# Another order of all engines' steps in a fused audio tower, with quad 0 as a token group of its own

## The reference, cut to what matters

```python
# token pooling: windows of 8 times, weighted by a softmax over the 8
scores  = einsum('bwkf,of->bwko', xp, w) + b          # xp: 128 x 94 x 8 x 64
pooled  = sum(xp * softmax(scores, axis=2), axis=2)   # 128 x 94 x 64
# attention, 8 heads, on layernorm(pooled)
q = einsum('btd,hrd->bhtr', x, Q);  k = einsum('bud,hrd->bhur', x, K)
attn = softmax(einsum('bhtr,bhur->bhtu', q, k) / sqrt(64))
out  = einsum('bhtd,hde->bte', einsum('bhtu,bud->bhtd', attn, x), VO)
# then an expert attention, causal, 4 heads x 4 experts of width 16,
# gated by a softmax over the experts, a small two-layer net per head
# between two normalisations, and a last gate over the heads
```

## Time and profile before

| | us |
|---|---|
| median of three runs (1001.07, 999.45, 999.99) | 999.99 |
| the profiled execution | 1001.54 |
| its span in the trace | 999.8 |
| a plain step in the middle, mix to mix | 27.0 |
| a step with a token score | 30.5 |
| from the start to the first `mix` | 56.0 |
| from the last `mix` to the end | 87.9 |

### The profile page before, as it was taken

One profiled execution on the slowest core, in us unless ns is written; L12 is line 12 of the kernel. 1 busy time (PEld: TensorE's weight loads), 2 busy tenths in 40 slices (PEclk: granted clock), 3 DMA queues, 4 the chain that ended last, 5 costly groups with the idle time before them and its releaser, 6 DMA issues.

```text
span 999.8 us, 39459 instructions
## 1 busy us (share of the span) xinstructions
PE 901.8 (90%) x16312; PEld 615.8 (62%) x16312; DVE 803.9 (80%) x1836; ACT 733.4 (73%) x2743; POOL 718.3 (72%) x1055
## 2 busy tenths in 40 slices
PE   4699999999999999999999999999999999998841
PEld 3365566666666667666676667666676666666630
DVE  2345678789879888889979888898989888888976
ACT  0456777788878887888878887888878888885520
POOL 2333235378877888688887888688887888888894
PEclk8687999999999999999999999999999999999985
DMA  7211111101111111011111111111100000000000
GB/s 196 72 33 40 40 41 41 29 22 36 38 45 45 45 44 44 14 43 43 37 44 45 45 44 44 24 35 43 42 7 14 14 13 14 13 14 13 16 7 20
DMA packets 40931, 36.48 MB, mean 36 GB/s; under 512 B 27312, under 2 KB 30512, under 8 KB 40752
## 3 DMA queue, kind: packets, MB, share of 16 engines
q1 hardware_dynamic: 40406, 33.91, 12.3%
q10 hardware_dynamic: 250, 0.05, 0.0%
q0 software_dynamic: 96, 0.00, 0.0%
HBM read 25.08 MB, written 3.08 MB: 28 GB/s over the span
## 4 chain that ended last, share of the span: by engine, by line
PE 68%; DVE 22%; ACT 5%; POOL 2%; issue 1%; DMA 1%; POOLq 0%; DVEq 0%
PE psum L778 8%; PE psum L699 7%; PE psum L689 7%; DVE pu L1431 6%; DVE mx L1428 6%; PE psum L727 6%; PE psum L804 5%; PE psum L763 5%; PE psum L681 4%; PE psum L610 4%; PE psum L707 4%; ACT pu L1120 3%; PE psum L623 3%; PE psum L793 3%; PE psum L631 3%; DVE mx L1399 2%
## 5 line engine op out<-in xcount | busy, mean ns | idle before, releaser
L1120 ACT ACTIVATE pu<-psum,mx 128x94 f32<-128x94 f32 x768 | 252.3, 401 | 6.5 <-DVE mx L1399 2.0
L1120 ACT ACTIVATION_READ_ACCUMULATOR pu<-psum,mx 128x1 f32 x768 | 202.5, 269 | 0.0
L1163 ACT ACTIVATE pT<-psum 96x512 f32<-96x512 f32 (+1 forms) x224 | 137.1, 613 | 65.2 <-PE psum L778 64.8
L778 PE MATMUL psum<-ident_w,pu 128*96 128x128 f32 (+1 forms) x896 | 141.6, 281 | 12.7 <-DVE ct L1439 10.5
L508 POOL TENSOR_TENSOR st<-st,neg_half 128x12 f32<-128x12 f32 x64 | 145.8, 2278 | 5.0
L474 POOL TENSOR_TENSOR pu<-pu,pr 128x752 f32<-128x752 f32 x96 | 138.5, 1447 | 13.4 <-DVE pr L1403 13.4
L1399 DVE TENSOR_REDUCE mx<-psum 128x8 f32<-128x752 f32 x96 | 89.4, 938 | 63.9 <-PE psum L689 63.1
L778 PEld LDWEIGHTS psum<-ident_w,pu 128*96 128x96 f32 (+1 forms) x896 | 95.4, 134 | 63.0 <-DVE ct L1439 31.7
L1428 DVE TENSOR_REDUCE mx<-psum 128x16 f32<-128x1536 f32 (+2 forms) x96 | 116.9, 1218 | 13.9 <-PE psum L763 13.2
L1431 DVE TENSOR_TENSOR pu<-psum,mx 128x1536 f32<-128x1536 f32 (+2 forms) x96 | 117.5, 1224 | 3.3
L804 PE MATMUL psum<-gx,ct 128*128 128x84 f32 x768 | 96.6, 275 | 4.3 <-ACT pu L1120 3.7
(11 more groups left out here) (184 smaller groups left out, 2170.4 us busy)
## 6 DMA issues: line engine op xcount, KB each, us to landing
xs<-in_x SPq DMA_DIRECT2D x64, 375.0 KB, 3.7
vb<-va SPq DMA_DIRECT2D x32, 128.0 KB, 2.2
out_h<-ho SPq DMA_DIRECT2D x126, 16.0 KB, 1.4
out_h<-ho SPq DMA_DIRECT2D x126, 7.5 KB, 1.4
vc<-va SPq DMA_DIRECT2D x96, 16.0 KB, 1.9
gx<-in_L_ffn_gate_w SPq DMA_DIRECT2D x16, 0.2 KB
fc<-in_L_ffn_fc_w SPq DMA_DIRECT2D x12, 1.0 KB
fc<-in_L_ffn_fc_b SPq DMA_DIRECT2D x12, 0.1 KB
```

What stands on the lines that cost most here:

```text
L778: mm = pe.transpose(psum[0:rows, bank, 128 * e:128 * e + 128], src, ident)
L1120: ins = act.activation(pu[:, j, par, hp, 0:NTOK], psum[:, (low, high)[par], NTOK * hp:NTOK * hp + NTOK], ACT.Exp, bias=mx[:, j, par, hp:hp ...
L1163: act.activation(pT3[j][:, f - (0, 4, 6)[i], :, :, :].rearrange("p e b t -> p (e b t)"), psum[0:rows, bank, :], ACT.Exp).then_inc(p_copied, 1)
```

## The change

- Token groups: quad 0 is scored alone (12 matmuls, two tiles), then quads 1 to 4, 5 to 8 and so on: nine groups for the eight before, the same matmuls in all. `tok_score` comes at the end of its step, behind `give_out` and ahead of the first `score3`.
- Loads: `tw`, `tokb`, then `q_w`, `k_w`, `vo_w`, then six of the experts' small loads (with a semaphore of their own, `ff_first`) go through ScalarE's queue. The other 53 stay on SyncE's behind the x loads.
- The order of all pieces, their distances and banks, on all five engines; the loops run from -3 to 12 in place of -1 to 11. On TensorE `give_outT`, `give_out` and the first `score3` come in one step, `mix3(0)` goes ahead of `give_out`, and the three scores use three pairs of banks, (3,4), (1,2) and (6,7). The first `score3` waits for `add_out` of the same step.
- Set-up: `make_g` stands between the first token score and `tok_turn`, `copy_g` ahead of `exp_tok`; `make_w` and `make_w2` stand ahead of the first `mix`.
- `sums(2)` stands behind the first `turn_p` on VectorE, and `norm_p(2)` is behind it on GpSimd.

```diff
-FF_LOADS = 16 * (6 * NH + 35)
+FF_LOADS = 16 * (6 * NH + 29)
+FF_FIRST = 16 * 6
...
-            sp.dma_start(q_w[:, :, :], attn_q.rearrange("h r d -> r h d")).then_inc(attn_loaded, 16)
...
+            act.wait_ge(padded, 1)
+            act.dma_start(tw[0:NFEAT, 30:31], tok_w.rearrange("o f -> f o")).then_inc(tok_loaded, 16)
...
+            act.dma_start(q_w[:, :, :], attn_q.rearrange("h r d -> r h d")).then_inc(attn_loaded, 16)
...
-                for p in range(2 * GQ):
+                pairs = range(max(0, -2 * n), min(2 * GQ, NPAIR - 2 * n))
+                for p in pairs:
...
-                pe.wait_ge(ff_loaded, FF_LOADS)
+                pe.wait_ge(ff_first, FF_FIRST)
...
+                pe.wait_ge(ff_loaded, FF_LOADS)
                 pe.wait_ge(causal_set, 10)
...
-            for q in range(-1, 12):
+            for q in range(-3, 13):
                 quad(q)
```

More of the change, by code:

```diff
@@ new lines, in quad @@
+                    if exists(g - 3, NQUAD):
+                        if g - 3 == 0:
+                            pe.wait_ge(f_resid, 1)
+                        else:
+                            pe.wait_ge(c_copied, 3 * g - 10)
+                    if exists(g - 6, NQUAD):
+                        layer1(4)
+                    if exists(g, NQUAD):
+                        turn_x(v % 4, 5)
+                    if exists(g - 3, NQUAD):
+                        turn_p3(3, 6)
+                        pe.wait_ge(p_copied, 7 * g - 20)
+                        turn_p3(2, 7)
+                        if exists(g, NQUAD):
+                            pe.wait_ge(at_xT, g + 1)
+                        else:
+                            pe.wait_ge(c_guarded, 3 * g - 9)
+                        turn_p3(0, 5)
@@ L938, in quad @@
[L938 to L948 removed]
+                            pe.wait_ge(at_exped, 3 * g - 2)
@@ L1020, in quad @@
+                    if exists(g - 3, NQUAD):
+                        turn_p3(6, 4)
+                    if exists(g, NQUAD):
+                        project(v % 2, 1, 7, 3)
+                    if g + 7 == 0:
+                        tok_score(-3, 7)
                     if exists(g - 1, NQUAD):
@@ L1070, in quad @@
                         else:
[L1071 to L1079 removed]
+                            pe.wait_ge(at_q, 4 * g + 3)
+                        score(v % 2, 2, 6, 7)
@@ new lines, in quad @@
+                    if exists(g - 3, NQUAD):
+                        mix3((v + 1) % 2, 0, 4)
+                    if exists(g + 2, NQUAD):
+                        turn(g + 2, 2, 5)
+                    if exists(g - 1, NQUAD):
+                        pe.wait_ge(at_oT, g)
+                        give_out(0)
+                    if g == 0:
+                        pe.wait_ge(at_exped, 3 * g + 1)
+                        make_w2(3)
+                    if exists(g + 4, NQUAD) and (g + 4) % 4 == 1:
+                        if g + 3 == 0:
+                            pe.wait_ge(tok_ready, 1)
+                        if exists(g - 3, NQUAD):
+                            pe.wait_ge(c_guarded, 3 * g - 7)
+                        elif exists(g, NQUAD):
+                            pe.wait_ge(at_exped, 3 * g + 1)
+                        tok_score(g + 4, 4)
@@ new lines, in quad @@
+                    if exists(g - 3, NQUAD):
+                        if exists(g + 2, NQUAD):
+                            pe.wait_ge(x_scaled, 3 * g + 8)
+                        else:
+                            pe.wait_ge(c_guarded, 3 * g - 8)
+                        turn_p3(5, 5)
+                        if exists(g + 4, NQUAD) and (g + 4) % 4 == 1:
+                            pe.wait_ge(tok_shifted, (g + 7) // 4 + 1)
+                        else:
+                            pe.wait_ge(c_guarded, 3 * g - 7)
+                        turn_p3(4, 4)
@@ L1309, in _ @@
-            for q in range(-1, 12):
+                            act.wait_ge(f_res, 1)
+                        front_res(6)
+                    if g + 9 == 0:
+                        exp_tok()
+                    if g + 4 == 0:
+                        if exists(g + 4, NQUAD):
+                            act.wait_ge(w_made, 1)
+                        copy_m(2)
+                    if exists(g - 2, NQUAD):
+                        act.wait_ge(r1_fxt, g - 1)
+                        copy_fxT(7)
@@ new lines, in quad @@
+                    if g + 12 == 0:
+                        if exists(g + 12, NQUAD):
+                            act.wait_ge(g_made, 1)
+                        copy_g(7)
+                    if exists(g + 3, NQUAD):
+                        copy_cT(0, 0)
+                    if exists(g + 6, NQUAD) and (g + 6) % 4 == 1:
+                        act.wait_ge(tok_turned, (g + 9) // 4 + 1)
+                        copy_tok(g + 6, 2)
+                    if exists(g + 4, NQUAD):
+                        act.wait_ge(at_maxed0, g + 5)
+                        exp_s(0, 3, 4)
@@ L1310, in _ @@
+                    if exists(g + 3, NQUAD):
+                        act.wait_ge(at_outT, g + 4)
+                        copy_oT(0)
+                    if exists(g + 4, NQUAD):
+                        act.wait_ge(at_maxed1, g + 5)
+                        exp_s(1, 1, 2)
+            for q in range(-3, 13):
                 quad(q)
@@ L1681, in _ @@
+                    if TAIL <= g - 12 < NQUAD:
+                        dve.wait_ge(fl_inv, 2 * g - 22)
+                        finish_late(g - 12, v % 2, (g - 12) // 2)
+            for q in range(-3, 13):
                 quad(q)
```

1002 lines of the change are left out of this document (468 added, 534 removed).

## The result

The changed kernel takes 1002.4 us (median of ten runs) against 999.4 for the kernel before: ratio 1.0032, interval 1.0020 to 1.0044. It is **slower by 0.3%**, where 988 had been forecast (974 to 1002).

The account below looks back on a forecast made before the run. TensorE, busy 90% of the span, was taken to bound the middle, and the chain through all engines the fill and drain. Fill -2, middle -7, drain -3 give -12: span 999.8 to 987.8, forecast 988.0 us, range 974 to 1002.

Parts of the forecast that it names:

- The idle time of the middle: TensorE waits over 29 middle steps: 0.8 us left in each of 23 plain steps, 0.2 in each of 6 token steps.
- the ring: First FFN score, VectorE's maximum and subtraction, second score: waits of 0.62 and 0.42 us go, a new 0.5 us comes.
- 26.0 of work: TensorE's work in a plain middle step; with 0.5 + 0.1 named and 0.2 unnamed waits, 26.8 us against 27.0.
- 29.5 us is all that another order can give there: Middle, 29 steps: TensorE's idle time, 800.6 - 771.1, taken as the most a reordering could save, since matmuls stay the same.
- -7: Middle: 0.2 us saved in each of 23 plain steps and 0.4 in each of 6 token steps; bounds -20 to +6.
- project at 21.9: Plain step on TensorE: project(0) starts 21.9 us after mix, just behind the earliest time of what it reads.
- The fill: Start of the span: first mix 2.0 us later, 4.7 off the stretch between first two mix, 0.7 for make_w2's copies: -2 us.
- the attention loads, put at 14.3: Fill: the last attention load, issued by ScalarE at 6.4, lands 7.9 us later, and make_g waits for it.
- make_w and make_w2: Fill: moving these set-up products (about 1 and 3.7 us) takes 4.7 us off the stretch between the first two mix.
- The drain: End of the span: last quad's score3(0) at mix + 24, not 26.9, turn_rest gives 0.6 back: -3 us, bounds -6 to +2.
- a rival of 0.14: Rival 1: the VectorE-GpSimd handover at norm_p(2) becomes the bound and delays mix; steps of 27.6, time 1012; chance 0.14.
- Rival 2: Nothing gained in the middle, new waits cost as much as the old 1.0; fill and drain give -5: 995; 0.14 with rival 5.

Follow-up runs that it names:

- b1_islands: Kernel before with layer2 moved on TensorE from behind the second score to between the first two scores: 1003.7 us, ratio 1.0036.
- x8_layer2: Changed kernel with give_out ahead of the third x turn, head_shift ahead of sums(2), layer2 behind both front_pair: 992.4 us, ratio 0.9925 to the kernel before.
- x1_swap_out: Changed kernel with give_out ahead of the third x turn on TensorE, not behind it: 999.5 us, ratio 0.9999 to the kernel before.
- m1_pieces: Kernel before with 96 unread pieces added at TensorE's end, alone and alternating: 0.15 to 0.17 us at each boundary between two shapes; no total time given.

## Why the prediction was wrong, point by point

- **The idle time of the middle** (19.6 us by the forecast's terms, 23 x 0.8 + 6 x 0.2): right, 18.5. The places and times of the ring were right to 0.1 us, but turn_c was put at 12.1 with nothing left over and comes at 12.4.
- **The step that failed: "26.0 of work", and before it "the matmuls of those steps are the same before and after, 29.5 us is all that another order can give there".** TensorE's busy time in a plain step went from 26.07 to 26.83. Counting the boundaries between shapes in one step (a piece whose successor starts 0.07 us ahead of its end; 0.16 or more where the shape stays, and from `128*96` to `128*128` too), the order before has 23 and the new one 26: 3 x 0.15 = 0.45. By the runs that moved a piece a boundary is 0.12 (b1_islands) to 0.20 (x8_layer2), so 0.35 to 0.6. Another 0.2 is the wait that the rows show as busy and x1_swap_out removes. About 0.1 is left unexplained. The step with tok_turn has 0.3 more, of `hxm` and a wait ahead of project(0) that was not in the forecast at all. Over 29 steps that is 18.4 us of busy time, against 11 us of waits saved: +7.3, where -7 stood. m1_pieces shows the price, b1_islands and x8_layer2 add and remove it; that the 0.45 are these three boundaries is a count, not a run of its own. I took each piece at one fixed price, although were read "by their length less the 0.07 of overlap", that is at the price of a boundary or not, as it fell.
- **project at 21.9, "just behind the earliest time of what it reads"**: 22.3, and mix at 27.4.
- **The fill** (-2 forecast): -6.6 in the two traces, -4.8 by the means of four. The first mix was put 2.0 later than before and comes 1.8 later by the means (at 56.5 in the trace of the changed kernel, 58.1 said), but not by the terms of the forecast: the attention loads, put at 14.3, landed at 18.2, and quad 0's turns began at 27.45, not 24.5. That the number came out is luck. The second interval, put at 20, is 18.9. make_w and make_w2 were the right term for that stretch (4 us, 4.7 said). The clock, higher in the fill of the changed kernel, was not in the forecast.
- **The drain** (-3 forecast): -0.7. Below, the maximum of the last quad and the last mix at 912.58: 26.3 us apart, where 24 was said and 26.9 stood. The 3 us for a softmax fewer between them did not come; why not, no run shows.

```profile
938.85 1.76 DVE L1452 TENSOR_REDUCE mx<-psum 128x16 f32<-128x1536 f32 x1 [0.46 <-PE psum L755]
```

- **Sum**: -6.6 + 7.3 - 0.7 = 0.0 between the two traces, 3.0 between the medians. With the fill by its means it is -4.8 + 7.3 - 0.7 = +1.8; the start of single traces scatters by 2 to 4 us, and the last 1.2 us are not placed.
- **Rivals.** The side that came true, slower, had a rival of 0.14 with the wrong mechanism: GpSimd was not late at norm_p(2): it waits there for `pr`. Its time was also added to 1000, not to the forecast's 988: with the step at 26.8 + 0.6 = 27.4 it would be 1005. What happened there instead was seen by none, VectorE held for 1.0 us by GpSimd; it cost nothing in a plain step and 0.3 us in the step with tok_turn. Rival 2, that the idle time comes back elsewhere, was nearest, but it came back as busy time.

## What to carry to other kernels

Price a piece of TensorE by its neighbours: a boundary between matmuls of different shape cost 0.12 to 0.20 us here, so an order that scatters the transposes among small tiles can lose more than the waits it hides. Before a wait is moved, find the two or three points that other engines fix (here turn_c, by ScalarE's exponentials after mix): a wait ahead of such a point is worth little (the 0.46 came back as 0.53; what x1_swap_out gained, 0.23, came from behind the point), one behind it was worth two thirds of what it lasted (0.2 to 0.3 of 0.32 to 0.42), and shortening the chain that fixes it half (0.13 of 0.24). Put a wait directly ahead of the piece that reads the data, not pieces earlier. Don't read the fill from one trace. A busy TensorE is no floor, and no wait row means no wait only where the successor does not start late.
